# Cross attention of a six-layer decoder: sequences taken in pairs, and the 257th key folded in as a shift

## The chip, the cores and the metric

The kernel runs on one core of a Trainium2 chip. The metric is device time in microseconds (us) of one launch; lower is better.

## The reference, cut to what matters

The program is a stack of twelve blocks over 32 sequences of 32 tokens with 256 features. The fourth block is a decoder of six layers, and the change lies in it alone:

```python
def mha(xq, xkv, W, B, mask):            # H = 16 heads of DH = 16
    q, k, v = proj(xq, W[0], B[0]), proj(xkv, W[1], B[1]), proj(xkv, W[2], B[2])
    score = jnp.einsum('bhqd,bhkd->bhqk', q, k) / math.sqrt(DH)
    if mask is not None:
        score = jnp.where(mask[:, None] == 0, -10000.0, score)
    attn = jax.nn.softmax(score, axis=-1)
    out = jnp.einsum('bhqk,bhkd->bhqd', attn, v)
    ...
    return out @ W[3] + B[3]

def step(x, p):                          # six times
    x = layer_norm(mha(x, x, saw, sab, mask) + x, ...)
    x = layer_norm(mha(x, enc, caw, cab, None) + x, ...)
    x = layer_norm(relu(x @ W1 + B1) @ W2 + B2 + x, ...)
```

`enc` is the context, 257 keys for each sequence (2 x 128 and one more). All is fp32.

## The kernel before, in words

`decoder_layers` writes out by hand one schedule for five engines. The 32 sequences are eight tiles of four sequences (128 token rows); with six layers that makes 48 positions. The schedule is a software pipeline: each step of its main loop works on four positions at once, one in self attention ("sa"), one in the projections of the context ("prep"), one in cross attention ("ca"), and one in the output projection and the MLP ("out", "dm"). A step has eight units, u = 0 to 7, one for each half of the heads (cc) and each sequence (j) of the "ca" position.

In each unit TensorE does, in this order: `scores` of the unit (into banks 0 and 1 of PSUM), `transposes` of the unit before (into bank 2), the jobs that `UNIT_JOBS[u]` lists, and `values` of the unit two before (into bank 3). Jobs take the four banks of a ring in turn; job n waits until job n-4's bank has been evacuated by the engine that the list names. The kinds of job named below: K and V project keys and values of the context, S0 to S7 are self attention's stages, D0 transposes the MLP's input, D1 and D2 are its first matmuls in two halves, D3 is its second matmul (it waits for ScalarE's evacuation of D1 and D2), Y is the output projection of cross attention, X and XK project the 257th value and key of all sequences once a layer.

VectorE (DVE in the rows) takes the maximum of each score row (`maxima`), evacuates its jobs (`take`), turns sums into reciprocals (`reciprocals`, every fourth unit), assembles heads (`own_heads`, u = 1 and 5) and does self attention's shift (`self_shift`, u = 3) and shares (`self_shares`, u = 4). ScalarE (ACT) does `exponentials`, then `copy_transposed` (bank 2 to SBUF), then its evacuations of the unit, among them D0's (one copy) and D1's and D2's (four activations each). Each engine works through its own list strictly in order, so a wait holds whatever stands behind it.

The wait that orders scores against the softmax, and the one that orders the second MLP matmul, read:

```python
need(pe, "exp_done", 2 * k)              # scores: banks 0 and 1 are read out
...
need_evacuated(pe, pos, "D1", 0)         # job D3
need_evacuated(pe, pos, "D2", 1)
```

## Time and profile before

| | |
|---|---|
| median of 3 runs | 4612.44 us (4609.56 to 4612.98) |
| profiled execution, its own time | 4595.03 us |
| its span | 4593.2 us |
| TensorE (PE) busy | 4045.7 us, 88% of the span |
| VectorE (DVE) busy | 2613.4 us, 57% |
| ScalarE (ACT) busy | 1853.6 us, 40% |
| GpSimd (POOL) busy | 300.9 us, 7% |
| mean granted TensorE clock | 0.937 of full speed |

Busy time is the time in which an engine has at least one instruction under way. PE is the matmul side of TensorE, PEld its weight loads. Instructions on TensorE overlap, so the time that one group takes from the queue is read from the start of the group to the start of the next, not from its own duration. A matmul in fp32 stands as two instructions in the trace. The decoder's score matmuls run from 774 to 2816 us of the span.

### The profile page before, as it was taken

To read this page: it belongs to the slowest core of one execution; us is meant where nothing else is said; L and a number is where in the kernel's file an instruction comes from. 1 tells how busy PE (TensorE), PEld (TensorE's weight loads), DVE (VectorE), ACT (ScalarE), POOL (GpSimd) and SP (SyncE) were. 2 spreads that over 40 slices of the span, in tenths; PEclk is the share of its full clock that TensorE was granted. 3 is DMA by queue.
4 is the path that set the end of the run, shared out by engine and by line. 5 is a ranking of instruction groups with operands and counts; after the bars stand their busy time and mean duration, and the time that the engine had idled before them with its cause. 6 is when DMAs were issued, how large, how long until landed. Compare 5 with 4: busy or idle time off the path is not lost. (4 is left out here: it accounts for less than half of the span.)

```text
span 4593.2 us, 105087 instructions
## 1 busy us (share of the span) xinstructions
PE 4045.7 (88%) x43842; PEld 3101.4 (68%) x43842; DVE 2613.4 (57%) x5580; ACT 1853.6 (40%) x5080; POOL 300.9 (7%) x560
## 2 busy tenths in 40 slices
PE   7988995999999999999999997779588787888867
PEld 6766884777777777777777775568345577566635
DVE  3435115777777777777777774721367654345545
ACT  1221221444444444444444443212266454255523
POOL 0000101000000000000000000010211000000000
PEclk9998997999999999999999998879799888888878
DMA  4110573011111111111111100048544300000000
GB/s 148 59 58 3 203 288 99 29 33 43 51 33 43 51 35 41 51 35 40 51 35 40 51 29 9 3 160 293 172 153 145 116 0 0 25 30 28 11 1 12
DMA packets 116921, 310.54 MB, mean 68 GB/s; under 512 B 29352, under 2 KB 75625, under 8 KB 92017
## 3 DMA queue, kind: packets, MB, share of 16 engines
q1 hardware_dynamic: 113392, 295.61, 18.8%
q0 software_dynamic: 3072, 8.39, 0.5%
q8 instruction: 342, 5.60, 0.5%
q14 instruction: 115, 0.93, 0.1%
HBM read 289.01 MB, written 14.94 MB: 66 GB/s over the span
## 5 line engine op out<-in xcount | busy, mean ns | idle before, releaser
L2490 ACT ACTIVATE layers_probs<-banks,layers_negmax 128x257 f32<-128x257 f32 x768 | 357.6, 471 | 1002.7 <-DVE layers_negmax L2369 1002.7
L2213 PE MATMUL banks<-ctx_tiles,weights_a 128*128 128x257 f32 x1536 | 397.4, 381 | 0.0
L2219 PE MATMUL banks<-weights_a,ctx_tiles 128*128 128x256 f32 x1536 | 379.4, 380 | 0.0
L2219 PEld LDWEIGHTS banks<-weights_a,ctx_tiles 128*128 128x128 f32 x1536 | 285.1, 191 | 35.4
L2369 DVE TENSOR_REDUCE layers_negmax<-banks 128x2 f32<-128x514 f32 x384 | 262.3, 683 | 71.5 <-PE banks L2274 71.5
L2213 PEld LDWEIGHTS banks<-ctx_tiles,weights_a 128*128 128x128 f32 x1536 | 270.9, 191 | 26.6 <-ACT layers_KT L2467 0.4
L2274 PE MATMUL banks<-layers_KT,layers_qblk 32*64 32x257 f32 x3072 | 256.2, 403 | 26.6 <-ACT layers_probs L2490 26.3
L2282 PEld LDWEIGHTS banks<-const,layers_probs 128*128 128x128 f32 x1536 | 162.2, 141 | 149.4 <-issue 149.3
L2282 PE MATMUL banks<-const,layers_probs 128*128 128x128 f32 x1536 | 253.6, 288 | 0.0
L2349 DVE TENSOR_TENSOR layers_V<-banks,rows_a 128x256 f32<-128x256 f32 x384 | 160.2, 418 | 138.8 <-PE banks L2219 132.9
L2495 ACT COPY layers_pT<-banks 128x512 f32<-128x512 f32 x384 | 223.5, 582 | 3.3 <-PE banks L2282 3.3
L2467 ACT ACTIVATE layers_KT<-banks,layers_ca_bk 128x257 f32<-128x257 f32 x384 | 184.2, 496 | 47.8 <-PE banks L2213 47.7
L2258 PE MATMUL banks<-layers_dm_nT,weights_b 128*128 128x128 f32 x1536 | 189.3, 277 | 0.6 <-ACT layers_dm_nT L2464 0.6
L2258 PEld LDWEIGHTS banks<-layers_dm_nT,weights_b 128*128 128x128 f32 x1536 | 184.8, 194 | 3.2 <-ACT layers_dm_nT L2464 0.9
L2263 PE MATMUL banks<-weights_b,layers_hid 128*128 128x256 f32 x768 | 173.8, 379 | 1.7 <-ACT layers_hid L2481 1.7
L2294 PEld LDWEIGHTS banks<-layers_pT,layers_V 128*32 128x32 f32 x6144 | 109.7, 109 | 87.8 <-issue 78.0
L2294 PE MATMUL banks<-layers_pT,layers_V 128*32 128x64 f32 x6144 | 163.6, 224 | 0.3 <-ACT layers_pT L2495 0.3
L2263 PEld LDWEIGHTS banks<-weights_b,layers_hid 128*128 128x128 f32 x768 | 145.7, 190 | 21.7 <-issue 2.1
L2490 ACT ACTIVATION_READ_ACCUMULATOR layers_probs<-banks,layers_negmax 128x1 f32 x768 | 150.6, 196 | 0.0
L2274 PEld LDWEIGHTS banks<-layers_KT,layers_qblk 32*64 32x64 f32 x3072 | 79.5, 130 | 96.4 <-issue 39.4
L2772 PE MATMUL banks<-weights_a,ctx_tiles 128*128 128x512 f32 x256 | 129.8, 636 | 1.0 <-DVE l2x_own L2847 0.5
L2345 DVE SCALAR_TENSOR_TENSOR weights_a<-banks,layers_sa_cols,const 128x1024 f32<-128x1024 f32 x96 | 118.4, 1274 | 7.3 <-PE banks L2206 7.3
(695 smaller groups left out, 8329.3 us busy)
## 6 DMA issues: line engine op xcount, KB each, us to landing
ctx_tiles<-in_ctx SPq DMA_DIRECT2D x65, 1028.0 KB, 5.1
weights_a<-in_L_w SPq DMA_DIRECT2D x44, 1024.0 KB, 5.4
l2x_B<-positions SPq DMA_DIRECT2D x32, 1280.0 KB, 5.9
weights_b<-in_L_w SPq DMA_DIRECT2D x32, 1024.0 KB, 6.2
weights_c<-in_L_w SPq DMA_DIRECT2D x16, 1024.0 KB, 7.1
weights_b<-in_L_xattn_w SPq DMA_DIRECT2D x12, 1024.0 KB, 7.4
l0x_key_rows<-in_ctx_rows SPq DMA_DIRECT2D x32, 256.0 KB, 2.7
ctx_tiles<-in_ctx_keys SPq DMA_DIRECT2D x32, 256.0 KB, 2.8
```

The costliest lines, as they stand in the source:

```text
L2213: last = mm(o[:, 0:LK], ca_wk[:, c, m * P:(m + 1) * P], E.ctx[:, tile % 2, c, j * LK:(j + 1) * LK], start=c == 0, stop=c == DC - 1)
L2219: last = mm(o[:, 0:D], E.ctx[:, tile % 2, c, first:first + P], ca_wv[:, c], start=c == 0, stop=c == DC - 1)
L2258: last = mm(o[:, i * P:(i + 1) * P], dm_w1[:, c, m * P:(m + 1) * P], dm_nT[:, c], start=c == 0, stop=c == DC - 1)
L2263: last = mm(o[:, 0:D], hid[:, m], dm_w2[:, m], start=m == 0, stop=m == FC - 1)
L2274: last = mm(ps[half, r // 2, 0:LK], qblk[rows, tile % 2, cc, j], KT[rows, tile % 2, cc, j * LK:(j + 1) * LK], start=True, stop=True)
L2282: last = tr(ps[:, TURN, (KC * t + c) * P:(KC * t + c + 1) * P], probs[:, cc, j, t, 1 + c * P:1 + (c + 1) * P], E.c("ident"))
L2294: last = mm(ps[32 * i:32 * (i + 1), PV, j * 64:(j + 1) * 64], V[:, pos % 2, KC * j + c, cc * P + 32 * i:cc * P + 32 * (i + 1)], pT[:, k % ...
L2349: last = v.tensor_tensor(V[:, tile % 2, arg], o[:, 0:D], E.rA[:, 0], ALU.add)
L2369: v.tensor_reduce(negmax[:, k % 2], ps[:, 0:2, 0:LK], AX.X, ALU.max, negate=True).then_inc(s["max_ready"], 1)
L2467: last = a(KT[:, pos % 2, m, j * LK:(j + 1) * LK], o[:, 0:LK], ACT.Identity, bias=ca_bk[:, m:m + 1])
L2490: a(probs[:, cc, j, t], ps[:, t, 0:LK], ACT.Exp, bias=negmax[:, k % 2, t:t + 1], accum_out=totals[:, cc, t, j:j + 1]).then_inc(s["exp_done ...
L2495: nc.scalar.copy(pT[:, k % 2].rearrange("p t c x -> p (t c x)"), ps[:, TURN]).then_inc(s["copied"], 1)
```

## The change

What it does:

- The key projections leave out the 257th key. It is projected once a layer for all sequences (job XK), and its projection is subtracted from every other key as the bias of the evacuation; the scores are then differences against the last key, whose own exponential is exp(-max), taken once for four sequences (`last_e`). The maximum is held at 0 or above by a second, tiny DVE instruction.
- K and V jobs cover two blocks of 256 columns each and fill a bank: four K and four V jobs a step instead of eight and eight.
- Scores, maxima and exponentials are done for two sequences at once, in even units. Transposes and values stay per sequence, but values of two sequences stand together in odd units. There are four buffers of `pT` instead of two.
- ScalarE's order in a unit is now `copy_transposed`, `exponentials` (even units: four of them, and in units 2 and 6 also `last_e`), evacuations. VectorE evacuates S6 in its own unit instead of in the next one, and takes put-off jobs ahead of `maxima`.

The diff, without the hunks that only rename what a semaphore waits for:

```diff
@@ -2042,2 +2042,3 @@
     VC = GB * KC
+    KW = KC * P
     U = DC * GB
...
@@ -2052,12 +2053,12 @@
     UNIT_JOBS = [
-        [k_job(0), v_job(0), k_job(1), v_job(1), ("S0", None, "act")],
-        [("S1q", None, "dve"), k_job(2), ("S1k", None, "act"), k_job(3), ("n", None, "act")],
-        [("q", None, "act"), k_job(4), ("Y", None, "dve"), ("S3", None, "dve")],
-        [k_job(5), v_job(2), k_job(6)],
-        [("D0", None, "act"), v_job(3), v_job(4), v_job(5)],
-        [("S2", None, "dve"), ("D1", 0, "act"), k_job(7), v_job(6), ("S6", None, "dve")],
-        [("D2", 1, "act"), v_job(7), ("X", None, "act")],
+        [("XK", None, "act"), ("S0", None, "act"), k_job(0), v_job(0)],
+        [("S1q", None, "dve"), k_job(1), ("S1k", None, "act"), ("n", None, "act")],
+        [("q", None, "act"), v_job(1), ("Y", None, "dve"), ("S3", None, "dve")],
+        [k_job(2), v_job(2)],
+        [("D0", None, "act"), k_job(3), ("S2", None, "dve")],
+        [("D1", 0, "act"), v_job(3), ("S6", None, "dve")],
+        [("D2", 1, "act"), ("X", None, "act")],
         [("S7", None, "dve"), ("D3", None, "dve")],
     ]
-    PART = {"n": "prep", "X": "prep", "q": "prep", "K": "prep", "V": "prep", "Y": "out", "S0": "sa", "S1q": "sa", "S1k": "sa", "S2": "sa", "S3": "sa", "S6": "sa", "S7": "sa",
+    PART = {"n": "prep", "X": "prep", "XK": "prep", "q": "prep", "K": "prep", "V": "prep", "Y": "out", "S0": "sa", "S1q": "sa", "S1k": "sa", "S2": "sa", "S3": "sa", "S6": "sa", "S7": "sa",
             "D0": "dm", "D1": "dm", "D2": "dm", "D3": "dm"}
...
@@ -2082,7 +2083,8 @@
         nT, qT, qblk = sb("nT", [DC, P]), sb("qT", [DC, P]), sb("qblk", [2, DC, GB, 2 * LQ])
-        KT, V = sb("KT", [2, DC, CT]), sb("V", [2, VC, D])
-        probs, pT = sb("probs", [DC, GB, 2, LK]), sb("pT", [2, 2, KC, P])
-        negmax, totals, spread = sb("negmax", [2, 2]), sb("totals", [2, 2, GB]), sb("spread", [2, 2, GB, LQ])
+        KT, V = sb("KT", [2, DC, GB * KW]), sb("V", [2, VC, D])
+        probs, pT = sb("probs", [DC, GB, 2, KW]), sb("pT", [4, 2, KC, P])
+        negmax, totals, spread = sb("negmax", [DC, 2, GB]), sb("totals", [2, 2, GB]), sb("spread", [2, 2, GB, LQ])
         blend, attnT = sb("blend", [2, GB, LQ]), sb("attnT", [DC, P])
         rates, last_v = sb("rates", [2, 2, GB]), sb("last_v", [2, DC, NB])
+        last_e, last_k, less_last = sb("last_e", [DC, 2, GB]), sb("last_k", [DC, NB]), sb("less_last", [2, DC, NB])
         sa_nT, sa_k, sa_v = sb("sa_nT", [DC, P]), sb("sa_k", [DC, P]), sb("sa_v", [GB, D])
...
@@ -2207,3 +2209,3 @@
                     elif kind == "K":
-                        m, j = arg
+                        m, i = arg
                         if arg == (0, 0):
@@ -2212,9 +2214,16 @@
                         for c in range(DC):
-                            last = mm(o[:, 0:LK], ca_wk[:, c, m * P:(m + 1) * P], E.ctx[:, tile % 2, c, j * LK:(j + 1) * LK], start=c == 0, stop=c == DC - 1)
+                            keys = E.ctx[:, tile % 2, c].rearrange("p (j k) -> p j k", j=GB)[:, 2 * i:2 * i + 2, 1:LK]
+                            last = mm(o.rearrange("p (j k) -> p j k", j=2), ca_wk[:, c, m * P:(m + 1) * P], keys, start=c == 0, stop=c == DC - 1)
                     elif kind == "V":
-                        first = arg // KC * LK + 1 + arg % KC * P
                         if arg == 0:
                             need_weights(pe, "w_ca_v", pos)
-                        for c in range(DC):
-                            last = mm(o[:, 0:D], E.ctx[:, tile % 2, c, first:first + P], ca_wv[:, c], start=c == 0, stop=c == DC - 1)
+                        for b in range(KC):
+                            first = arg * LK + 1 + b * P
+                            for c in range(DC):
+                                last = mm(o[:, b * D:(b + 1) * D], E.ctx[:, tile % 2, c, first:first + P], ca_wv[:, c], start=c == 0, stop=c == DC - 1)
+                    elif kind == "XK":
+                        need_weights(pe, "w_ca_k", pos)
+                        for m in range(DC):
+                            for c in range(DC):
+                                last = mm(o[:, m * NB:(m + 1) * NB], ca_wk[:, c, m * P:(m + 1) * P], E.last[:, c], start=c == 0, stop=c == DC - 1)
                     elif kind == "X":
@@ -2269,7 +2278,8 @@
                         pe.wait_ge(s["qblk_ready"], pos + 1)
-                        need_evacuated(pe, pos, "K", (DC - 1, GB - 1))
+                        need_evacuated(pe, pos, "K", (DC - 1, 1))
                     need(pe, "exp_done", 2 * k)
-                    for r in (0, 2, 1, 3):
-                        rows, half = slice(32 * r, 32 * (r + 1)), slice(64 * (r % 2), 64 * (r % 2 + 1))
-                        last = mm(ps[half, r // 2, 0:LK], qblk[rows, tile % 2, cc, j], KT[rows, tile % 2, cc, j * LK:(j + 1) * LK], start=True, stop=True)
+                    for a in range(2):
+                        for r in (0, 2, 1, 3):
+                            rows, half = slice(32 * r, 32 * (r + 1)), slice(64 * (r % 2), 64 * (r % 2 + 1))
+                            last = mm(ps[half, r // 2, a * KW:(a + 1) * KW], qblk[rows, tile % 2, cc, j + a], KT[rows, tile % 2, cc, (j + a) * KW:(j + a + 1) * KW], start=True, stop=True)
                     last.then_inc(s["scores_done"], 1)
...
@@ -2290,6 +2300,6 @@
                         if cc == 0:
-                            need_evacuated(pe, pos, "V", VC - 1)
+                            need_evacuated(pe, pos, "V", GB - 1)
                     for c in range(KC):
                         for i in range(4):
-                            last = mm(ps[32 * i:32 * (i + 1), PV, j * 64:(j + 1) * 64], V[:, pos % 2, KC * j + c, cc * P + 32 * i:cc * P + 32 * (i + 1)], pT[:, k % 2, i // 2, c, 64 * (i % 2):64 * (i % 2 + 1)], start=c == 0, stop=c == KC - 1)
+                            last = mm(ps[32 * i:32 * (i + 1), PV, j * 64:(j + 1) * 64], V[:, pos % 2, KC * j + c, cc * P + 32 * i:cc * P + 32 * (i + 1)], pT[:, k % 4, i // 2, c, 64 * (i % 2):64 * (i % 2 + 1)], start=c == 0, stop=c == KC - 1)
                     last.then_inc(s["pv_done"], 1)
@@ -2302,10 +2312,11 @@
                 for it in range(N * U):
-                    if ca_unit(it):
+                    if it % 2 == 0 and ca_unit(it):
                         scores(*ca_unit(it))
-                    if ca_unit(it - 1):
-                        transposes(*ca_unit(it - 1))
+                    if ca_unit(it - 2):
+                        transposes(*ca_unit(it - 2))
                     for a in jobs_in(it):
                         job(*a)
-                    if ca_unit(it - 2):
-                        values(*ca_unit(it - 2))
+                    for back in (3, 2):
+                        if it % 2 and ca_unit(it - back):
+                            values(*ca_unit(it - back))
 
...
@@ -2367,4 +2378,6 @@
                 def maxima(k, pos, cc, j):
-                    dve.wait_ge(s["scores_done"], k + 1)
-                    v.tensor_reduce(negmax[:, k % 2], ps[:, 0:2, 0:LK], AX.X, ALU.max, negate=True).then_inc(s["max_ready"], 1)
+                    dve.wait_ge(s["scores_done"], k // 2 + 1)
+                    peak = negmax[:, cc, :, j:j + 2]
+                    link(v.tensor_reduce(peak, ps[:, 0:2].rearrange("p t (a x) -> p t a x", a=2), AX.X, ALU.max, negate=True))
+                    v.tensor_scalar(peak, peak, 0.0, None, ALU.min).then_inc(s["max_ready"], 1)
 
@@ -2372,4 +2385,6 @@
                     need(dve, "exp_done", 2 * (k + 1))
-                    link(v.reciprocal(rates[:, :, 0], totals[:, cc]))
-                    link(v.tensor_tensor(rates[:, :, 1], rates[:, :, 0], probs[:, cc, :, :, 0].rearrange("p j t -> p t j"), ALU.mult))
+                    dve.wait_ge(s["last_exp"], k // GB + 1)
+                    link(v.tensor_tensor(rates[:, :, 0], totals[:, cc], last_e[:, cc], ALU.add))
+                    link(v.reciprocal(rates[:, :, 0], rates[:, :, 0]))
+                    link(v.tensor_tensor(rates[:, :, 1], rates[:, :, 0], last_e[:, cc], ALU.mult))
                     v.tensor_tensor(spread[:].rearrange("p t s j q -> p (t s j) q"), E.c("pick").unsqueeze(1).to_broadcast([P, 4 * GB, LQ]),
@@ -2417,4 +2432,2 @@
                     step, u = it // U, it % U
-                    if ca_unit(it):
-                        maxima(*ca_unit(it))
                     for a in put_off:
@@ -2422,4 +2435,6 @@
                     put_off.clear()
+                    if it % 2 == 0 and ca_unit(it):
+                        maxima(*ca_unit(it))
                     for a in jobs_in(it):
-                        if a[3] in ("S3", "S6", "D3"):
+                        if a[3] in ("S3", "D3"):
                             put_off.append(a)
@@ -2465,4 +2480,15 @@
                     elif kind == "K":
-                        m, j = arg
-                        last = a(KT[:, pos % 2, m, j * LK:(j + 1) * LK], o[:, 0:LK], ACT.Identity, bias=ca_bk[:, m:m + 1])
+                        m, i = arg
+                        for j in (2 * i, 2 * i + 1):
+                            seq = pos % NG * GB + j
+                            last = a(KT[:, pos % 2, m, j * KW:(j + 1) * KW], o[:, j % 2 * KW:(j % 2 + 1) * KW], ACT.Identity, bias=less_last[:, pos // NG % 2, m, seq:seq + 1])
+                    elif kind == "XK":
+                        for m in range(DC):
+                            a(last_k[:, m], o[:, m * NB:(m + 1) * NB], ACT.Identity, bias=ca_bk[:, m:m + 1]).then_inc(s["last_keys"], 1)
+                        act.wait_ge(s["last_keys"], DC * (pos // NG + 1))
+                        for m in range(DC):
+                            last = a(less_last[:, pos // NG % 2, m], last_k[:, m], ACT.Identity, scale=-1.0, bias=ca_bk[:, m:m + 1])
+                        last.then_inc(s["evac_act"], 1)
+                        need_evacuated(act, pos, "XK")
+                        return
                     elif kind == "q":
@@ -2484,8 +2510,11 @@
                 def exponentials(k, pos, cc, j):
-                    act.wait_ge(s["max_ready"], k + 1)
-                    need(act, "transposed", k - U + 1)
+                    act.wait_ge(s["max_ready"], k // 2 + 1)
+                    need(act, "transposed", k + 1 - U + 1)
                     if j == 0:
                         need(act, "spread_ready", k // GB - 1)
-                    for t in range(2):
-                        a(probs[:, cc, j, t], ps[:, t, 0:LK], ACT.Exp, bias=negmax[:, k % 2, t:t + 1], accum_out=totals[:, cc, t, j:j + 1]).then_inc(s["exp_done"], 1)
+                    for i in (j, j + 1):
+                        for t in range(2):
+                            a(probs[:, cc, i, t], ps[:, t, i % 2 * KW:(i % 2 + 1) * KW], ACT.Exp, bias=negmax[:, cc, t, i:i + 1], accum_out=totals[:, cc, t, i:i + 1]).then_inc(s["exp_done"], 1)
+                    if j == GB - 2:
+                        a(last_e[:, cc], negmax[:, cc], ACT.Exp).then_inc(s["last_exp"], 1)
 
@@ -2493,4 +2522,4 @@
                     act.wait_ge(s["transposed"], k + 1)
-                    need(act, "pv_done", k - 1)
-                    nc.scalar.copy(pT[:, k % 2].rearrange("p t c x -> p (t c x)"), ps[:, TURN]).then_inc(s["copied"], 1)
+                    need(act, "pv_done", k - 3)
+                    nc.scalar.copy(pT[:, k % 4].rearrange("p t c x -> p (t c x)"), ps[:, TURN]).then_inc(s["copied"], 1)
 
@@ -2498,6 +2527,6 @@
                     step, u = it // U, it % U
-                    if ca_unit(it):
+                    if ca_unit(it - 2):
+                        copy_transposed(*ca_unit(it - 2))
+                    if it % 2 == 0 and ca_unit(it):
                         exponentials(*ca_unit(it))
-                    if ca_unit(it - 1):
-                        copy_transposed(*ca_unit(it - 1))
                     for b in jobs_in(it):
```

Two places of the order. First ScalarE in unit 4 (the copy out of bank 2, the exponentials, the evacuation of D0 to `dm_nT`, then D1's to `hid`). Before:

```order
L2507 ACTIVATE layers_sa_sc<-layers_sa_sc 128x512
L2490 ACTIVATE layers_probs,layers_totals<-banks,layers_negmax 128x257 x2
L2495 COPY layers_pT<-banks 128x512
L2464 COPY layers_dm_nT<-banks 128x256
L2490 ACTIVATE layers_probs,layers_totals<-banks,layers_negmax 128x257 x2
L2495 COPY layers_pT<-banks 128x512
L2481 ACTIVATE layers_hid<-banks,layers_dm_cols 128x128 x4
```

And in the changed kernel, through unit 6, where the second half of the MLP's hidden layer (D2) is evacuated:

```order
L2536 ACTIVATE layers_sa_sc<-layers_sa_sc 128x512
L2524 COPY layers_pT<-banks 128x512
L2517 ACTIVATE layers_probs,layers_totals<-banks,layers_negmax 128x256 x4
L2479 COPY layers_dm_nT<-banks 128x256
L2484 ACTIVATE layers_KT<-banks,layers_less_last 128x256 x2
L2524 COPY layers_pT<-banks 128x512
L2507 ACTIVATE layers_hid<-banks,layers_dm_cols 128x128 x4
L2524 COPY layers_pT<-banks 128x512
L2517 ACTIVATE layers_probs,layers_totals<-banks,layers_negmax 128x256 x4
L2519 ACTIVATE layers_last_e<-layers_negmax 128x8
L2507 ACTIVATE layers_hid<-banks,layers_dm_cols 128x128 x4
```

D0's evacuation stood behind two exponentials and a copy, and stands behind four exponentials; D2's stood behind two and a copy, and stands behind five.

Second VectorE from unit 5 to the maxima of unit 6 (V's evacuation, S6's in L2357 and L2360 of before, own heads from L2386 of before on, the maximum). Before:

```order
L2349 TENSOR_TENSOR layers_V<-banks,rows_a 128x256
L2386 TENSOR_SCALAR layers_blend<-banks,const 128x128
L2387 TENSOR_TENSOR layers_blend<-banks,layers_last_v 128x128
L2388 SCALAR_TENSOR_TENSOR layers_blend<-banks,const,layers_blend 128x128
L2389 TENSOR_TENSOR layers_blend<-banks,layers_blend 128x128
L2390 TENSOR_TENSOR layers_attnT<-layers_blend 128x128
L2369 TENSOR_REDUCE layers_negmax<-banks 128x2
L2357 TENSOR_SCALAR layers_sa_blend<-banks,const,layers_sa_bv 128x128 x2
L2360 SCALAR_TENSOR_TENSOR layers_sa_attnT<-banks,const,layers_sa_blend 128x128 x2
```

In the changed kernel:

```order
L2360 TENSOR_TENSOR layers_V<-banks,rows_a 128x512
L2368 TENSOR_SCALAR layers_sa_blend<-banks,const,layers_sa_bv 128x128 x2
L2371 SCALAR_TENSOR_TENSOR layers_sa_attnT<-banks,const,layers_sa_blend 128x128 x2
L2401 TENSOR_SCALAR layers_blend<-banks,const 128x128
L2402 TENSOR_TENSOR layers_blend<-banks,layers_last_v 128x128
L2403 SCALAR_TENSOR_TENSOR layers_blend<-banks,const,layers_blend 128x128
L2404 TENSOR_TENSOR layers_blend<-banks,layers_blend 128x128
L2405 TENSOR_TENSOR layers_attnT<-layers_blend 128x128
L2381 TENSOR_REDUCE layers_negmax<-banks 128x2x2
L2382 TENSOR_SCALAR layers_negmax<-layers_negmax 128x2x2
```

S6's four instructions moved from behind unit 6's maximum to ahead of it, and the maximum covers twice the columns.

## Rows read from the trace of the kernel before

**Rows 1.** Windows, decoder: us; PE, PEld, DVE, ACT, POOL busy (count), clock, DMA share, GB/s.

```profile
774.00:2816.00 2042.00, 1988.19 (x22373) 1527.14 (x22372) 1471.12 (x3283) 939.86 (x3045) 115.90 (x280) 1.00 0.12 39
```

**Rows 2.** Timeline of one step, PE: start us, us, engine, line, operation.

```profile
1716.93 0.66 PE L2274 MATMUL banks<-layers_KT,layers_qblk 32*64 32x257 f32 x8
...
1727.43 0.44 PE L2199 MATMUL banks<-const,h_state 128*128 128x128 f32 x2 [0.51 <-DVE weights_a L2345]
...
1727.79 0.43 PE L2294 MATMUL banks<-layers_pT,layers_V 128*32 128x64 f32 x16
...
1728.04 0.62 PE L2299 MATMUL banks<-layers_spread,const 128*32 128x256 f32 x8
...
1738.21 0.66 PE L2274 MATMUL banks<-layers_KT,layers_qblk 32*64 32x257 f32 x8 [0.39 <-ACT layers_probs L2490]
...
1738.80 0.66 PE L2282 MATMUL banks<-const,layers_probs 128*128 128x128 f32 x4
...
1739.52 2.76 PE L2219 MATMUL banks<-weights_a,ctx_tiles 128*128 128x256 f32 x12
...
1742.20 0.43 PE L2294 MATMUL banks<-layers_pT,layers_V 128*32 128x64 f32 x16
...
1742.56 0.66 PE L2274 MATMUL banks<-layers_KT,layers_qblk 32*64 32x257 f32 x8
...
1748.12 1.10 PE L2246 MATMUL banks<-layers_sa_pT,layers_sa_v 128*32 128x64 f32 x64
...
1750.90 1.95 PE L2258 MATMUL banks<-layers_dm_nT,weights_b 128*128 128x128 f32 x16
...
1759.86 0.66 PE L2274 MATMUL banks<-layers_KT,layers_qblk 32*64 32x257 f32 x8
```

**Rows 3.** Timeline of the same step, DVE.

```profile
1737.96 0.77 DVE L2403 COPY_PREDICATED_SCALAR layers_sa_sc<-mask_zero,layers_floor 128x512 f32 x1
...
1740.09 0.68 DVE L2369 TENSOR_REDUCE layers_negmax<-banks 128x2 f32<-128x514 f32 x1
...
1746.63 1.21 DVE L2351 TENSOR_TENSOR layers_sa_v<-banks,const 128x1024 f32<-128x1024 f32 x1
...
1750.02 0.35 DVE L2386 TENSOR_SCALAR layers_blend<-banks,const 128x128 f32<-128x128 f32 x1 [1.36 <-PE banks L2299]
...
1751.53 0.68 DVE L2369 TENSOR_REDUCE layers_negmax<-banks 128x2 f32<-128x514 f32 x1
...
1752.13 0.72 DVE L2357 TENSOR_SCALAR layers_sa_blend<-banks,const,layers_sa_bv 128x128 f32<-128x128 f32 x2
...
1752.88 0.61 DVE L2360 SCALAR_TENSOR_TENSOR layers_sa_attnT<-banks,const,layers_sa_blend 128x128 f32<-128x128 f32 x2
```

**Rows 4.** Timeline of the same step, ACT.

```profile
1742.19 0.39 ACT L2464 COPY layers_dm_nT<-banks 128x256 f32<-128x256 f32 x1
...
1752.24 0.48 ACT L2490 ACTIVATE layers_probs<-banks,layers_negmax 128x257 f32<-128x257 f32 x1 [2.60 <-DVE layers_negmax L2369]
...
1753.16 0.58 ACT L2495 COPY layers_pT<-banks 128x512 f32<-128x512 f32 x1
...
1753.62 1.16 ACT L2481 ACTIVATE layers_hid<-banks,layers_dm_cols 128x128 f32<-128x128 f32 x4
```

**Rows 5.** Timeline, PE, the decoder's first step, two waits.

```profile
780.19 0.44 PE L2199 MATMUL banks<-const,h_state 128*128 128x128 f32 x2 [1.75 <-ACT layers_KT L2467]
...
804.93 1.10 PE L2246 MATMUL banks<-layers_sa_pT,layers_sa_v 128*32 128x64 f32 x64 [1.53 <-DVE layers_sa_v L2351]
```

**Rows 6.** Windows around those two waits, columns as in rows 1.

```profile
777.40:780.90 3.50, 1.75 (x15) 0.98 (x13) 1.94 (x5) 1.99 (x7) 0.00 (x0) 1.00 0.00 0
780.90:784.30 3.40, 3.40 (x21) 2.95 (x14) 0.78 (x2) 1.64 (x6) 0.00 (x0) 0.50 0.00 0
802.40:805.80 3.40, 1.87 (x67) 1.44 (x69) 2.75 (x4) 1.87 (x6) 0.00 (x0) 1.00 0.00 0
805.80:809.20 3.40, 3.29 (x73) 1.95 (x62) 2.29 (x7) 0.17 (x1) 0.00 (x0) 1.00 0.02 5
```

16 lines of the change are left out of this document (8 added, 8 removed).

## The prediction, made before the changed kernel ran

> **What bounds the kernel now.** I read the page first, then the windows over the decoder, the timeline of one step on each engine, and the waits. In the decoder TensorE has work under way for 1988 of 2042 us at full clock; DVE stands at 1471 and ACT at 940 [rows 1]. One step goes from the scores at 1716.93 to those at 1759.86, 42.93 us, and there are 48. Inside it TensorE waits twice: 0.51 us for DVE before a transpose and 0.39 us for exponentials before scores [rows 2]. So TensorE's own queue sets the step, and ACT's and DVE's chains fit behind it. The decoder gains where that queue gets shorter, and loses where one of those chains, made longer, comes out ahead of it.
>
> All sums are against the profiled execution (span 4593.2, its own time 4595.0 us); the median of the runs is 4612.4, 17 us more. I add the change to the median.
>
> **What gets shorter on TensorE.** The columns stay: leaving out the 257th saves one column in 257. What goes is switching between shapes. Single `values` take 0.36 us to the scores behind them (1742.20 to 1742.56), and 0.25 where the next matmuls have the same shape (1727.79 to 1728.04) [rows 2]; so two `values` in a row take about 0.36 + 0.22 = 0.58 instead of 0.72, and entering the shape from wide matmuls, about 0.1, is paid once instead of twice. Scores take 0.59 (1738.21 to 1738.80). Their eight instructions run four abreast, two waves; two more waves cost at least the column rate, 0.22 each (12 instructions of 256 columns in 2.68 us with one switch, 1739.52 to 1742.20), and at most another 0.59: a pair is 1.03 to 1.18, and I take 1.03, since the added waves have no switch. Transposes behind wide matmuls lose about 0.06. Per pair: 0.15 + 0.14 + 0.1 + 0.06 = 0.45, per step 1.8 us. Both waits of before are in units whose order changes; I take them as gone, 0.9, and 0.15 for the restart (estimate). The least here is 1.2 us (scores without gain), the most 2.85.
>
> Here a rule can be set against the rows. K's 16 matmuls of 257 columns become 8 of 512. Sixteen instructions of 128 columns take 1.95 us, 12 of 256 columns 2.68 [rows 2]: twice the columns, twice the time, so the number of instructions is worth next to nothing and I count nothing. The Trainium skill (TensorEngine Tiling (Array Packing), Instruction Overhead) gives each matmul about 60 cycles of overhead; by it the 16 instructions saved in a step would give another 0.4 us, and the forecast would be some 19 us lower. The rows decide.
>
> XK adds 8 instructions once a layer, which load 128 columns each: about 0.11 us apiece as in [rows 2] (1750.90), 0.9 us, 5 us over six layers. The tiny new operations on DVE and ACT (minimum, `last_e`, one more in `reciprocals`) cost some 0.2 us each on engines with room, except where they stand in the chains below.
>
> **What gets longer: two chains.** Pair maximum: 1024 columns take DVE 1.21 us (1746.63) [rows 3]; with the minimum chained behind it, 1.42 from its start to its release. ACT starts 0.03 later (1751.53 + 0.68 against 1752.24), and two exponentials take 0.92 (1752.24 to 1753.16) [rows 3, 4], so four take 1.84. Before, an evacuation stood behind two; now it stands behind all four, and these behind a maximum twice as long.
>
> *Unit 4, D0 to D1.* Count from the start of unit 4's scores. V2's evacuation ends at about +0.15 (it begins about with the `values` ahead and covers 512 columns). Then comes self attention's shift, 2.13 us (1737.96 to 1740.09) [rows 3], to +2.27, and only then the maximum: released +3.69, exponentials +3.72 to +5.56, D0's copy 0.39 [rows 4] to +5.95, TensorE released at +6.00. TensorE itself is there earlier: scores 1.03, transposes and D0 0.72 (1738.80 to 1739.52), K 1.72, S2 0.86, unit 5's transposes 0.44, in all 4.77 [rows 2]. D1 waits 1.23 us. In the old order D0's copy had two exponentials ahead of it, and three V jobs, values, the next scores and S2 stood between D0 and D1 on TensorE; now it is K3 and S2.
>
> *Unit 6, D2 to D3.* Count from the start of unit 6's scores. S6's last result comes 0.18 after the `values` behind it start (1748.12 + 1.10) [rows 2], about 0.8 us before the scores. Its evacuation, 1.36 us (1752.13 to 1753.49), no longer waits until after the maximum; it ends at +0.59. Own heads take 1.51 (1750.02 to 1751.53) [rows 3]: +2.10. Maximum and minimum +3.52, exponentials +3.55 to +5.39, `last_e` +5.54, D2's four activations 1.16 [rows 4] to +6.70, D3 may start at +6.75. TensorE is there at 1.03 + 0.50 + 1.78 (D2) + 0.44 + 0.86 (S7) = +4.61. D3 waits 2.14 us. V7, which stood in unit 6, is gone from there. Behind D3 on TensorE are `values` and the next step's scores, so nothing gives this time back.
>
> The other waits I went through hold: S1q behind S0's copy has 0.7 us to spare, K2 behind q's evacuation 0.3 us (late next, if anything is), S6 behind self attention's shares 0.2 us. The context loads start earlier than before, with V3 in unit 5. No weight transfer is moved in SP's queue, and the weights of K are asked for in unit 5, many us ahead of XK.
>
> Sum per step: -1.8 - 1.05 + 1.23 + 2.14 = +0.5 us, 48 times 25 us; with XK about +29 us: 4641.
>
> **The clock.** A wait of some 2 us has a second price. In the decoder's first step TensorE waited 1.75 us, then ran at a granted clock of 0.50, that is 1.2 GHz, for the next 3.4 us; after a wait of 1.53 us in a stretch just as dense it stayed at 1.00, 2.4 GHz [rows 5, 6]. D3's wait has 2.14 us by starts, 1.97 idle. I expect it to cost the clock in some steps and not in others, since the drop comes at moments of its own, not at once. 3.4 us at half speed lose 1.7 us of TensorE's work, and D3, 16 matmuls without a pause, stands right there. Half of the steps: 24 times 1.7, another 41 us. Together +70: **4682 us**.
>
> The Trainium skill (TensorE: Matmul & The Clock Gate, Why this matters for your kernels) accepts idle gaps longer than this one between bursts; by it the clock would hold and the time be 4641. The wait of 1.75 us in the rows speaks against it.
>
> **The rivals.**
> 1. *Both waits, the clock falls after many of the long ones* (forecast): 4682, chance 0.42. Its own range 4655 to 4715.
> 2. *Both waits, the clock holds.* 4641 (4622 to 4655), chance 0.25. For it: 1.97 us is an estimate, with an error of some 0.4, and 1.53 did no harm.
> 3. *The waits are there but smaller, about what TensorE saves:* new waits of 2.6 to 2.95 us in a step instead of 3.4, and no loss of clock. 4605 to 4622, chance 0.10.
> 4. *Faster:* TensorE's shorter queue wins. The mechanism would be one place: D3 finds D2's evacuation done early, because own heads and the maximum in unit 6 start sooner than I reckon (if S6's evacuation and own heads cost 0.8 us less than their rows). The point from which it decides: new waits under 2.55 us in a step. With D3's wait at 1.2 us the step gains 0.42 us, 20 us in all, less 5 for XK: 4597. If both waits vanished, -2.85 x 48 + 5 = -132 us: 4480. Chance 0.13; for it speaks that the work saved is certain and the waits are worked out, against it that 0.8 us must be found.
> 5. *The clock falls in nearly every step,* or a pair of scores costs 1.18 and q's evacuation comes late too: 48 times 1.7 us, 4723, and with 0.3 us a step more 4738. Chance 0.10.
>
> About 0.2% (9 us) is what a measurement of this kernel can tell from no change: slower 0.77, within it 0.10, faster 0.13. The range leaves out the far ends of cases 4 and 5: 4598 to 4730.
>
> **What the profile would show.** Right: in each of the 48 steps a wait of D1's matmuls for `dm_nT` and one of D3's for `hid`, near 1.2 and 2 us; stretches of 3.4 us at clock 0.50 within the decoder, most of them behind D3's wait; four score groups of 16 instructions to a step with 1.03 us to the next group; none of the old waits before transposes and scores. Wrong: TensorE without waits, or steps shorter than 42.9 us. My weakest points are the length of D3's wait, which rests on a chain of seven durations, and the number of steps in which the clock falls.

## The result, and the profile after

The changed kernel takes 4680.99 us (median of 4 runs, 4672.28 to 4687.78), the kernel before 4611.00 in the same comparison (4 runs): a ratio of 1.0152 with a 95% interval of 1.0133 to 1.0172, 70 us slower. The forecast was 4682, slower.

The page of the profiled execution of the changed kernel (its own time 4682.26 us): span, then busy time and share of the engines, then the granted clock in 40 slices.

```profile
span 4680.5 us, 103588 instructions
...
PE 4025.6 (86%) x43122; PEld 3004.6 (64%) x43122; DVE 2628.4 (56%) x5484; ACT 1875.9 (40%) x5200; POOL 300.4 (6%) x560
...
PEclk9998997999999999999999998969799888888878
```

TensorE works 20 us less than before and the span is 87 us longer. Not all of the 87 us belong to the change. This is the decoder's first matmul, with the wait ahead of it:

```profile
737.92 0.66 PE L2201 MATMUL banks<-const,h_state 128*128 128x128 f32 x2 [33.79 <-PEq L201]
```

In the trace of before the same instruction starts at 726.87, so 11 us of the difference between these two executions lie ahead of the decoder, where nothing was changed, and 6 us lie behind it. From the first step's scores to the 48th step's it is 2077.3 us against 2014.1, +63.2; the decoder's start and end add about 7. That makes the 70 us of the medians.

One step on TensorE, from the end of unit 2 to unit 1 of the next step (start us, us, engine, line, operation; it answers to [rows 2]):

```profile
1728.67 1.07 PE L2247 MATMUL banks<-weights_a,layers_sa_k 128*32 128x256 f32 x16
1729.67 0.66 PE L2292 MATMUL banks<-const,layers_probs 128*128 128x128 f32 x4
...
1734.29 1.09 PE L2284 MATMUL banks<-layers_KT,layers_qblk 32*64 32x256 f32 x16
1735.31 0.66 PE L2292 MATMUL banks<-const,layers_probs 128*128 128x128 f32 x4
...
1736.02 1.88 PE L2216 MATMUL banks<-ctx_tiles,weights_a 128*128 128x512 f32 x4
1737.74 1.03 PE L2241 MATMUL banks<-weights_c,layers_sa_nT 128*128 128x256 f32 x4
1738.61 0.60 PE L2292 MATMUL banks<-const,layers_probs 128*128 128x128 f32 x4
1740.35 2.02 PE L2267 MATMUL banks<-layers_dm_nT,weights_b 128*128 128x128 f32 x16 [1.15 <-ACT layers_dm_nT L2479]
...
1745.94 1.09 PE L2284 MATMUL banks<-layers_KT,layers_qblk 32*64 32x256 f32 x16
...
1749.68 1.03 PE L2260 MATMUL banks<-weights_c,layers_sa_attnT 128*128 128x256 f32 x4
1752.64 5.38 PE L2272 MATMUL banks<-weights_b,layers_hid 128*128 128x256 f32 x16 [1.93 <-ACT layers_hid L2507]
1757.95 0.66 PE L2304 MATMUL banks<-layers_pT,layers_V 128*32 128x64 f32 x32
1758.54 1.09 PE L2284 MATMUL banks<-layers_KT,layers_qblk 32*64 32x256 f32 x16
```

The reader is to see: a pair of scores (L2284) leaves TensorE's queue after 1.02 us; in unit 5 the transposes at 1738.61 are followed by nothing until D1 (L2267) at 1740.35; in unit 7 S7 (L2260) starts at 1749.68 and D3 (L2272) only at 1752.64, after 1.93 us idle; and D3's 16 instructions then take 5.31 us to the values behind them, where they took 3.62 in other steps.

VectorE in the same step (answers to [rows 3]):

```profile
1736.56 1.22 DVE L2381 TENSOR_REDUCE layers_negmax<-banks 128x4 f32<-128x1024 f32 x1
1737.81 0.17 DVE L2382 TENSOR_SCALAR layers_negmax<-layers_negmax 128x4 f32<-128x4 f32 x1
...
1745.21 0.73 DVE L2368 TENSOR_SCALAR layers_sa_blend<-banks,const,layers_sa_bv 128x128 f32<-128x128 f32 x2 [0.38 <-PE banks L2255]
...
1746.49 0.34 DVE L2401 TENSOR_SCALAR layers_blend<-banks,const 128x128 f32<-128x128 f32 x1
...
1747.99 1.22 DVE L2381 TENSOR_REDUCE layers_negmax<-banks 128x4 f32<-128x1024 f32 x1
```

ScalarE in the same step (answers to [rows 4]):

```profile
1738.02 0.47 ACT L2517 ACTIVATE layers_probs<-banks,layers_negmax 128x256 f32<-128x256 f32 x1 [0.24 <-DVE layers_negmax L2382]
...
1739.83 0.38 ACT L2479 COPY layers_dm_nT<-banks 128x256 f32<-128x256 f32 x1
...
1749.44 0.47 ACT L2517 ACTIVATE layers_probs<-banks,layers_negmax 128x256 f32<-128x256 f32 x1 [1.20 <-DVE layers_negmax L2382]
...
1751.35 1.15 ACT L2507 ACTIVATE layers_hid<-banks,layers_dm_cols 128x128 f32<-128x128 f32 x4
```

Both chains can be read off. Unit 4: the maximum starts at 1736.56, 2.27 us behind the scores at 1734.29; it is released at 1737.98; four exponentials take from 1738.02 to 1739.83; D0's copy (`dm_nT`) ends at 1740.21, and D1 starts at 1740.35. Unit 6: S6's evacuation (1745.21) and own heads (1746.49) come ahead of the maximum at 1747.99, 2.05 us behind the scores at 1745.94; the exponentials start at 1749.44, D2's evacuation (`hid`) ends at 1752.50, D3 starts at 1752.64.

The window behind D3's start (busy us and count of PE, PEld, DVE, ACT, POOL, then clock, DMA share and GB/s), and who TensorE waited for between the first and the last step:

```profile
1753.80:1757.20 3.40, 3.40 (x9) 2.66 (x8) 0.80 (x2) 0.00 (x0) 0.00 (x0) 0.50 0.36 90
```

```profile
PE banks L2272 <- ACT layers_hid L2507: 78.0, 45, 1.9
PE banks L2267 <- ACT layers_dm_nT L2479: 46.8, 41, 1.2
...
PE banks L2309 <- issue: 4.1, 3, 1.4
PE banks L2284 <- issue: 2.4, 3, 1.2
```

Two waits stand where before there were none. D1's is there in 46 of the 47 intervals between steps, at 1.10 to 1.15 us idle in all but the last (in five of them, left out of the lines above, another releaser is named). D3's is 1.93 us idle in 34 intervals and mostly shorter in the others, where a layer begins or TensorE was late for another reason. A granted clock of 0.50, that is 1.2 GHz, stands right behind D3's start in 13 of these 34; such an interval is 45.41 us long, a plain one 43.72. The kernel before has 42.93 in all but the first two, the last and the five with a new layer.

### The profile page after: what moved, and what is told of

It reads as the page before. It is cut to its first block and busy times, and to the rows that moved or that the text cites. A ratio compares the mean times of both kernels' runs of the same rounds, so it can differ in the third digit from the quotient of the medians.

```text
span 4680.5 us, 103588 instructions
## 1 busy us (share of the span) xinstructions
PE 4025.6 (86%) x43122; PEld 3004.6 (64%) x43122; DVE 2628.4 (56%) x5484; ACT 1875.9 (40%) x5200; POOL 300.4 (6%) x560
## 3 DMA queue, kind: packets, MB, share of 16 engines
q1 hardware_dynamic: 113392, 295.61, 18.5%
## 5 line engine op out<-in xcount | busy, mean ns | idle before, releaser
L2517 ACT ACTIVATE layers_probs<-banks,layers_negmax 128x256 f32<-128x256 f32 x768 | 353.2, 472 | 134.7 <-DVE layers_negmax L2382 134.7
L2216 PE MATMUL banks<-ctx_tiles,weights_a 128*128 128x512 f32 x768 | 363.4, 596 | 0.0
L2272 PE MATMUL banks<-weights_b,layers_hid 128*128 128x256 f32 x768 | 200.8, 421 | 84.2 <-ACT layers_hid L2507 84.2
L2360 DVE TENSOR_TENSOR layers_V<-banks,rows_a 128x512 f32<-128x512 f32 x192 | 132.6, 691 | 241.8 <-PE banks L2223 241.8
L2267 PE MATMUL banks<-layers_dm_nT,weights_b 128*128 128x128 f32 x1536 | 195.1, 282 | 55.5 <-ACT layers_dm_nT L2479 50.0
L2272 PEld LDWEIGHTS banks<-weights_b,layers_hid 128*128 128x128 f32 x768 | 158.3, 211 | 126.1 <-issue 86.9
L2381 DVE TENSOR_REDUCE layers_negmax<-banks 128x4 f32<-128x1024 f32 x192 | 233.9, 1218 | 6.5 <-PE banks L2284 3.1
L2484 ACT ACTIVATE layers_KT<-banks,layers_less_last 128x256 f32<-128x256 f32 x384 | 163.9, 486 | 158.6 <-PE banks L2216 158.6
L2267 PEld LDWEIGHTS banks<-layers_dm_nT,weights_b 128*128 128x128 f32 x1536 | 183.3, 196 | 65.7 <-DVE layers_sa_v L2362 60.8
L2284 PE MATMUL banks<-layers_KT,layers_qblk 32*64 32x256 f32 x3072 | 213.0, 390 | 2.6 <-issue 2.4
L2216 PEld LDWEIGHTS banks<-ctx_tiles,weights_a 128*128 128x128 f32 x768 | 131.9, 192 | 92.8 <-issue 92.8
L2284 PEld LDWEIGHTS banks<-layers_KT,layers_qblk 32*64 32x64 f32 x3072 | 98.8, 132 | 78.2 <-issue 45.3
L2507 ACT ACTIVATE layers_hid<-banks,layers_dm_cols 128x128 f32<-128x128 f32 x384 | 109.9, 378 | 54.5 <-PE banks L2267 54.5
L2304 PE MATMUL banks<-layers_pT,layers_V 128*32 128x64 f32 x6144 | 126.4, 223 | 4.0 <-ACT layers_pT L2524 4.0
```

The lines of the kernel that those rows point to most:

```text
L2216: last = mm(o.rearrange("p (j k) -> p j k", j=2), ca_wk[:, c, m * P:(m + 1) * P], keys, start=c == 0, stop=c == DC - 1)
L2267: last = mm(o[:, i * P:(i + 1) * P], dm_w1[:, c, m * P:(m + 1) * P], dm_nT[:, c], start=c == 0, stop=c == DC - 1)
L2272: last = mm(o[:, 0:D], hid[:, m], dm_w2[:, m], start=m == 0, stop=m == FC - 1)
L2284: last = mm(ps[half, r // 2, a * KW:(a + 1) * KW], qblk[rows, tile % 2, cc, j + a], KT[rows, tile % 2, cc, (j + a) * KW:(j + a + 1) * KW], ...
L2304: last = mm(ps[32 * i:32 * (i + 1), PV, j * 64:(j + 1) * 64], V[:, pos % 2, KC * j + c, cc * P + 32 * i:cc * P + 32 * (i + 1)], pT[:, k % ...
L2360: last = v.tensor_tensor(V[:, tile % 2, KC * arg:KC * (arg + 1)], o.rearrange("p (b d) -> p b d", b=KC), E.rA[:, 0].unsqueeze(1).to_broadc ...
```

## The experiments

Ratios are to the kernel before, timed on the same chip. The chips differ between groups of rows, so two ratios whose intervals overlap are told apart by the traces, not by the ratios. "Steps" is the time from the first step's scores to the 48th step's in the profiled execution, "plain step" the most frequent interval among those without a D3 at half clock. Expectations given as times are on the footing of the result, where the kernel before took 4611 us; a measured ratio times 4611 can be held against them.

| kernel | ratio (95% interval) | plain step, us | steps, us |
|---|---|---|---|
| before | 1 | 42.93 | 2014.1 |
| changed | 1.0152 (1.0133 to 1.0172) | 43.72 | 2077.3 |
| first evacuation first, unit 4 only | 1.0144 (1.0124 to 1.0165) | 43.46 | 2069.9 |
| S7 twice | 1.0124 (1.0103 to 1.0145) | 43.73 | 2059.6 |
| S6 put off | 1.0104 (1.0087 to 1.0121) | 43.40 | 2048.3 |
| heads late | 1.0037 (1.0022 to 1.0051) | 42.86 | 2022.9 |
| first evacuation first, unit 6 only | 0.9939 (0.9919 to 0.9959) | 41.81 | 1980.0 |
| first evacuation first, all even units | 0.9880 (0.9855 to 0.9905) | 41.55 | 1956.0 |
| both orders mended, values single | 0.9808 (0.9786 to 0.9829) | 41.03 | 1926.7 |
| both orders mended | 0.9768 (0.9752 to 0.9784) | 40.42 | 1897.8 |

### ScalarE's order, in all even units

```diff
+                    own = [b for b in jobs_in(it) if b[5] == "act"]
+                    early = own[:1] if u in (0, 2, 4, 6) else []
+                    for b in early:
+                        take(*b)
                     if it % 2 == 0 and ca_unit(it):
                         exponentials(*ca_unit(it))
-                    for b in jobs_in(it):
+                    for b in own[len(early):]:
                         take(*b)
```

Expected: 

> The changed kernel, but ScalarE takes the first evacuation of an even unit ahead of the pair's exponentials. Theory (ScalarE's order makes both waits, 1.3 us before D1 and 2.1 us before D3): both waits go and with D3's wait the loss of clock. D1's wait comes back in part as a wait of S6 for self attention's shares on VectorE, about 1.1 us, because in the changed kernel these were ready only 0.2 us ahead of S6. Step 43.72 - 0.2 - 2.1 = 41.4 us, total 4681 - 110 - 27 (clock) = about 4544. If nothing replaces D1's wait: 4490. Rival (the later, longer maximum on VectorE holds the step, whatever ScalarE's order is): the exponentials, now later still, hold scores or transposes, and the step stays near 43.7, total 4670 or more.

Measured: ratio 0.9880 (4556 us on the footing of the expectation), plain step 41.55 us. The largest waits of TensorE from the second step on:

```profile
PE banks L2255 <- DVE layers_sa_pT L2427: 46.8, 44, 1.2
PE banks L2267 <- issue: 1.4, 1, 1.4
```

D1's wait is gone, D3's is 0.18 us by starts, and S6 (L2255) waits 1.1 us for self attention's shares, as worked out. No D3 ran at half clock. The exponentials, now later in units 4 and 6, hold no matmul in these steps. The rival falls.

### The same in unit 4 alone, and in unit 6 alone

```diff
-                    early = own[:1] if u in (0, 2, 4, 6) else []
+                    early = own[:1] if u in (4,) else []
```

These lines are against the experiment above. In the second kernel the last line has `(6,)`.

Expected for unit 4: 

> Only in unit 4 the evacuation of D0 goes ahead of the exponentials. Theory: D1's wait of 1.3 us goes, a wait of about 1.1 us stands before S6, the step gains 0.2 us, D3's wait and the loss of clock stay: 4671. Rival (each wait is a cost of its own): the step gains 1.3 us, 62 us in all: 4619.

Measured: ratio 1.0144 (4677 us on that footing), plain step 43.46, 0.26 us less.

```profile
PE banks L2272 <- ACT layers_hid L2507: 81.2, 45, 2.5
PE banks L2255 <- DVE layers_sa_pT L2427: 46.7, 44, 1.2
```

D1's wait is gone and S6's is there in its place; D3's (L2272) is unchanged. D3 is at half clock in 19 steps here, 13 in the changed kernel, with the same wait ahead of it: six times 1.69 us, which takes back 10 of the 12 us that 0.26 us a step give. Removing the shorter wait alone gives next to nothing: VectorE's queue stands right behind it, and the clock fell more often.

Expected for unit 6: 

> Only in unit 6 the evacuation of D2 goes ahead of the exponentials. Theory: D3's wait of 2.1 us goes and no D3 runs at half clock, D1's wait stays: 4681 - 101 - 27 = 4553. Rival (the clock falls for another reason than D3's wait): 4681 - 101 = 4580, with slow stretches left.

Measured: ratio 0.9939 (4583 us on that footing), plain step 41.81, 1.91 us less.

```profile
PE banks L2267 <- ACT layers_dm_nT L2479: 45.8, 40, 1.2
PE banks L2309 <- issue: 5.9, 4, 1.8
```

D3's wait falls from 2.10 us by starts to 0.18 (D2's evacuation still ends a little late), D1's stays, and no D3 runs at half clock. The time lies 30 us above the theory's 4553 and beside the rival's 4580; what excludes the rival is the trace, which has no slow stretch left behind the first step. The steps got 97 us shorter, where 1.91 x 47 and 22 us for the clock make 112. The 15 us that are missing: the pauses of TensorE that the last section tells of lengthen the steps by 13 us here and by 5 in the changed kernel, where D3's wait swallowed part of them; the five steps with a new layer lose 3 us in the same way, and the first interval is 1.7 us longer here.

Units 4 and 6 alone gain 0.26 and 1.91 us, all even units together 2.17: units 0 and 2, where the order was changed too, add nothing.

### More work inside D3's wait

```diff
-                        for c in range(DC):
-                            last = mm(o[:, 0:D], sa_attnT[:, c], sa_wo[:, c], start=c == 0, stop=c == DC - 1)
+                        for again in range(2):
+                            for c in range(DC):
+                                last = mm(o[:, 0:D], sa_attnT[:, c], sa_wo[:, c], start=c == 0, stop=c == DC - 1)
```

Expected: 

> The matmuls of S7 are done twice into the same bank, 0.87 us of idle work for TensorE that lies within D3's wait; the result is the same. Theory (D3's wait of 2.1 us costs the clock): the wait falls to 1.2 us, step lengths stay at 43.72 but no step has a D3 at half clock: 4681 - 27 = 4654. Rival 1 (the clock falls whatever TensorE's pause is): 4681. Rival 2 (added work is paid in full): 4681 + 42 = 4723.

Measured: ratio 1.0124 (4668 us on that footing), plain step 43.73. TensorE's waits, and D3's instructions in this kernel and in the changed one (min/median/max ns):

```profile
PE banks L2268 <- ACT layers_dm_nT L2480: 45.8, 40, 1.2
PE banks L2273 <- ACT layers_hid L2508: 41.1, 44, 1.1
```

```profile
L2273 PE MATMUL banks<-weights_b,layers_hid x720: 379/379/454, 860.3 to 2798.6; 128*128 128x256 f32 x180
```

```profile
L2272 PE MATMUL banks<-weights_b,layers_hid x720: 379/379/671, 867.9 to 2826.6; 128*128 128x256 f32 x180
```

With 0.87 us of extra matmuls in each step the 48 steps took 17.7 us less (one profiled execution each; the intervals of the two ratios overlap by a little). The plain step is as long as in the changed kernel, the wait is 1.1 us idle instead of 1.9, and in this window no D3 instruction comes near the 671 ns that the slowest took at half clock. The one D3 behind the window, in the last step, waited 2.47 us idle and did run at half clock. By this the loss of clock is an effect of D3's long wait, and it cost 22 us (13 times 1.69), not the 27 that the expectation had counted with. Both rivals fall: the first by the trace, since the time lies midway between it and the theory, the second by the step.

### VectorE's part in D3's wait

Own heads behind unit 6's maximum:

```diff
                     if it % 2 == 0 and ca_unit(it):
                         maxima(*ca_unit(it))
+                    if u == 6 and ca_unit(it - 3):
+                        own_heads(*ca_unit(it - 3))
...
-                    if ca_unit(it - 2) and (it - 2) % GB == GB - 1:
+                    if u == 1 and ca_unit(it - 2):
                         own_heads(*ca_unit(it - 2))
```

Expected: 

> The changed kernel, but VectorE assembles the first half's heads after unit 6's maximum instead of before it (ScalarE's order as in the changed kernel). Theory (VectorE's 1.5 us of own heads and S6's evacuation stand in the chain to D3's wait): the maximum starts 0.95 us earlier, D3's wait falls from 2.1 to 1.2 us, no D3 at half clock: -46 - 27 us against the changed kernel, ratio to before 0.999. Rival (the wait comes from ScalarE's order alone, VectorE is not in it): D3's wait and the clock stay, ratio 1.015.

Measured: ratio 1.0037, plain step 42.86, 0.86 us less where 0.95 was expected, and no D3 at half clock. The ratio came out above the 0.999 expected: the steps got 54 us shorter, not 73. The clock gave back 22 us and not 27, the wait 40 and not 46, and pauses lengthen the steps by 11 us here, 5 in the changed kernel.

```profile
PE banks L2267 <- ACT layers_dm_nT L2481: 47.0, 41, 1.2
PE banks L2272 <- ACT layers_hid L2509: 43.2, 45, 1.1
```

S6's evacuation behind unit 6's maximum, as before the change:

```diff
+                    late = [a for a in put_off if a[3] == "S6"]
                     for a in put_off:
-                        take(*a)
+                        if a[3] != "S6":
+                            take(*a)
                     put_off.clear()
                     if it % 2 == 0 and ca_unit(it):
                         maxima(*ca_unit(it))
+                    for a in late:
+                        take(*a)
                     for a in jobs_in(it):
-                        if a[3] in ("S3", "D3"):
+                        if a[3] in ("S3", "S6", "D3"):
```

Expected: 

> The changed kernel, but S6's evacuation on VectorE stands behind unit 6's maximum again, as in the kernel before. Theory: own heads start 0.45 us earlier, D2's evacuation ends 0.45 us earlier; S7 on TensorE now waits about 0.7 us for S6's evacuation, and D3 about 1 us after it, both within the same span. The step gains 0.45 us (22 us in all), and with two short waits instead of one of 2.1 us no D3 runs at half clock, another 27: ratio to before 1.004. Rival (the clock falls as often): 1.010. Rival (S6's place is of no account): 1.015.

Measured: ratio 1.0104, plain step 43.40: 0.32 us less, where 0.45 was expected.

```profile
PE banks L2272 <- ACT layers_hid L2511: 31.9, 45, 0.7
PE banks L2260 <- DVE layers_sa_attnT L2371: 23.0, 36, 0.7
```

The one wait is split in two of 0.65 and 0.72 us, and no D3 of the steps ran at half clock. The forecast of 1.004 missed: 29 us were gained in the steps, not 49. The ratio is that of the first rival (the clock falls as often), but the trace excludes it. Both runs together say that VectorE's queue ahead of the maximum is part of D3's wait, but moving it can't undo it: the exponentials alone keep D2's evacuation back.

### Both orders mended

Self attention's shares ahead of the reciprocals, on top of ScalarE's order:

```diff
+                    if u == 4 and steps[step]["sa"] is not None:
+                        self_shares(steps[step]["sa"])
                     if ca_unit(it - 1):
                         if (it - 1) % GB == GB - 1:
                             reciprocals(*ca_unit(it - 1))
...
-                    if u == 4 and steps[step]["sa"] is not None:
-                        self_shares(steps[step]["sa"])
```

Expected: 

> Both: ScalarE takes the first evacuation of an even unit ahead of the exponentials, and VectorE does self attention's shares in unit 4 ahead of the reciprocals. Theory (with D1's wait gone, the 1.1 us that S6 waits are VectorE's queue in unit 4, and the reciprocals' 1.25 us ahead of the shares make them): no wait before S6, step 41.55 - 1.1 = 40.45 us, time 53 us under that of the kernel with the order of ScalarE alone, a ratio to the kernel before of 0.976 to 0.977. Rival (the reciprocals, now later, hold the matmuls that spread them in unit 5): the wait only moves there, ratio 0.988.

Measured: ratio 0.9768, plain step 40.42. TensorE's waits of over 0.15 us from the second step on, of which there is one, and five rows of units 5 to 7:

```profile
PE banks L2272 <- ACT layers_hid L2507: 0.9, 1, 0.9
```

```profile
1704.42 1.95 PE L2267 MATMUL banks<-layers_dm_nT,weights_b 128*128 128x128 f32 x16
1706.21 1.89 PE L2223 MATMUL banks<-weights_a,ctx_tiles 128*128 128x256 f32 x8
1708.03 1.10 PE L2255 MATMUL banks<-layers_sa_pT,layers_sa_v 128*32 128x64 f32 x64
...
1713.68 1.03 PE L2260 MATMUL banks<-weights_c,layers_sa_attnT 128*128 128x256 f32 x4
1714.73 3.69 PE L2272 MATMUL banks<-weights_b,layers_hid 128*128 128x256 f32 x16
```

This is the change as it could have been: 2.3% faster than the kernel before, and 3.8% faster than the changed one, from two changes of order that touch no instruction's work. What was between is seen here as its absence: D1 at 1704.42 to V3 to S6 without a gap, and 1.05 us from S7 to D3 instead of 2.96.

### What the fewer changes of shape are worth

```diff
-                    for back in (3, 2):
-                        if it % 2 and ca_unit(it - back):
-                            values(*ca_unit(it - back))
+                    if ca_unit(it - 2):
+                        values(*ca_unit(it - 2))
```

Expected: 

> The kernel with both orders mended (ScalarE's first evacuation ahead, self attention's shares ahead of the reciprocals), step 40.42 us without a wait, but the values of each sequence stand in their own unit again instead of two together in odd units. Same matmuls, only more changes of shape. Theory (TensorE's gain in the changed kernel is fewer changes of shape): 0.14 us for each of four pairs, about 0.1 for entering the shape from wide matmuls in units 0, 4 and 6 and about 0.06 for leaving it there, together 1.0 us a step, 48 us: ratio to the kernel before 0.987. Rival (changes of shape cost nothing beyond the matmuls; the gain came from elsewhere): step 40.4, ratio 0.977.

Measured: ratio 0.9808, plain step 41.03: 0.61 us more than with values in pairs, where 1.0 was expected.

```profile
1712.13 0.43 PE L2304 MATMUL banks<-layers_pT,layers_V 128*32 128x64 f32 x16
1712.49 0.66 PE L2292 MATMUL banks<-const,layers_probs 128*128 128x128 f32 x4
...
1717.40 0.43 PE L2304 MATMUL banks<-layers_pT,layers_V 128*32 128x64 f32 x16
1717.76 1.09 PE L2284 MATMUL banks<-layers_KT,layers_qblk 32*64 32x256 f32 x16
```

The values at 1712.13 take 0.36 us to the transposes behind them, and the values ahead of scores 0.36, as in the kernel before. So changes of shape cost time, and the rival falls. Laid side by side, the two traces show which of the four pairs saves: joining unit 0's values with unit 1's, and unit 4's with unit 5's, is worth 0.3 us each, as expected. Unit 2's are worth nothing, since they stand behind S3, which has their shape already: S3 takes 0.89 us to the values, and 1.01 to the transposes when the values are gone. Of unit 6's next to nothing is left, since with pairs TensorE reaches D3 earlier and waits there for D2's evacuation, 0.18 us by starts.

## Why the prediction was right, point by point

**What bounds the kernel.** TensorE's queue set the step; this held. With both orders mended only D3's 0.18 us are left and the step is 40.42 us, all but the changed queue's own length.

**What TensorE saves.** A pair of scores took 1.02 us (1.03 forecast) and a pair of values 0.58 to 0.59 (0.58). The sum of 1.8 us a step was too high. S3 is now followed by transposes instead of values, a change of shape that was not there before (1.00 us from S3 at 1728.67 to the transposes, 0.89 to the values before), and entering the values from wide matmuls is spared in three units of four. From 42.93, less 1.13 for the old waits by starts, to 40.42 less the 0.18 that D3 still waits there, it is 1.56 us. This term of the sum was mis-sized, by 0.24 us a step.

**The number of instructions.** Four K instructions of 512 columns take 1.72 us (1736.02 to 1737.74), as eight of 257 did. Columns are what is paid for here; the 0.4 us a step that the Trainium skill's overhead for each matmul (TensorEngine Tiling (Array Packing), Instruction Overhead) would have given, by estimate, are not there.

**Unit 4, D0 to D1.** Forecast 1.23 us, measured 1.31 by starts (1.74 from the transposes, of which they take 0.44). Maximum to release 1.42 (1.42), exponentials 1.81 (1.84). The experiment in unit 4 shows that ScalarE's order makes this wait, and that the 0.2 us named as S6's room behind the shares were about right: it gained 0.26.

**Unit 6, D2 to D3.** Forecast 2.14 us, measured 2.10 by starts. ScalarE's order makes it: mended in unit 6 alone, the kernel is faster than before. On VectorE, putting S6's evacuation behind the maximum takes 0.32 us off the step, putting own heads there 0.86.

**The clock.** That some of these waits cost the clock and others not was right, and the price too, 1.69 us (1.7). The number was half of the forecast: 13 intervals, not 24, so 22 us instead of 41.

**The sum.** The plain step grew by 0.79 us where 0.52 was forecast: 37 us in all against 25. The clock took 22 us against 41. XK, forecast at 5 us, took next to nothing: the step in which a layer begins is 0.84 us longer than a plain one, 0.81 in the kernel before, for its matmuls lie inside D3's wait, which is 1.08 us idle there (where D3 hardly waits, a layer's step is 1.44 us longer). Two terms were not in the forecast at all: the pauses of the last section, 5 us, and the decoder's start and end, 7 us. The total of 4682 against 4681 is right to a microsecond by luck, because these errors cancel; its parts are right to about 20 us.

**The rivals.** The second (the clock holds) lies 40 us below the measured time and is excluded by the half-clock stretches. The third falls with it: the new waits are 3.41 us by starts in a plain step, above its 2.95. The fifth is excluded by the 13 intervals and by the pair of scores at 1.02 us. Of the fourth: own heads moved out of the chain do what it says to D3's wait (1.23 us by starts), and the time still came out 0.37% above the kernel before, not below. The plain step is 0.07 us shorter than before where it forecast 0.42: TensorE saves 1.56 us and not 1.8, and the waits are a little longer. The pauses, 11 us, more than undo that.

## What to carry to other kernels

When work is done in pairs, each engine's turn at it is twice as long, and what stands behind it in that engine's list gets twice as late: put the short evacuation that the busiest engine waits for ahead of the long batch. It cost 2.7% here to do it the other way round, on an engine that is busy 40% of the time, and 3.8% together with one more place of the same kind on VectorE.

When a wait is removed, look at what was due just behind it: D1's wait gave back 0.26 of its 1.31 us until VectorE's order was mended as well. And a wait of about 2 us on TensorE may cost more than itself, since the clock can fall behind it (13 times in 34 here); filling it with matmuls that nobody needs made the decoder's steps shorter.

## What the runs showed of the hardware that was not expected

The clock falls behind some of several equal waits. D3 waits 1.93 us idle in 34 steps of the changed kernel, and 13 of them are followed by half clock; with unit 4 alone mended it is 19 of 37. At 1.0 to 1.1 us idle (S7 twice, heads late) no D3 had it. Between the two, a pause of 1.70 us in the second step of the kernel with all even units mended was followed by half clock, and one of 1.75 us in the same place with unit 4 alone mended was not. Which waits it falls behind doesn't look like chance: the fall comes 0.1 to 1.1 us after D3's start, and in the kernel with unit 4 alone mended the first five of these distances are 0.40, 0.54, 0.64, 0.78 and 0.92 us, the next five 0.14, 0.23, 0.36, 0.50 and 0.53. Nothing was run to find out what decides.

TensorE also pauses where the profile names no releaser, in a few steps, often in the middle of a run of equal instructions:

```profile
1258.67 0.59 PE L2309 MATMUL banks<-layers_spread,const 128*32 128x256 f32 x3
1260.61 0.63 PE L2309 MATMUL banks<-layers_spread,const 128*32 128x256 f32 x5 [1.35 <-issue]
```

In the changed kernel there are seven such pauses with 6.9 us together between the first and last step, in the one with unit 6 alone mended seven with 8.8 us. S7 twice has six, heads late eight, S6 put off seven, the two in which unit 4's order is mended (unit 4 only, all even units) three each; the kernel before and the two with both orders mended have none. It is not an accident of one execution: in the changed kernel, the one with unit 6 alone mended, heads late and S6 put off, pauses stand in the same six intervals, counted from the first step: numbers 8, 21 and 34, and 11, 24 and 37, each time 13 apart.

The trace has one thing that stands ahead of every one of them. The page lists a DMA queue named `instruction` (packets, MB, share); its packets have 16 KB each:

```profile
q8 instruction: 337, 5.52, 0.5%
```

The pause above ends at 1260.61; the last packet of this queue before it ran from 1257.91 to 1259.05, and the one before that had come 20.8 us earlier, where the median distance in this kernel is 11.9. All 41 pauses of the seven kernels end 1.2 to 1.6 us after such a packet has landed, and the packet came 16.8 to 20.8 us after the one before. In the three kernels without pauses no distance from the second step on is above 18.5 us. So it looks as if TensorE had run out of instructions; that is read from these times, and was not tested. Why the packets come late in these steps stays open. In 35 of the 41 the load of the next context tile had been issued in the 7 us before; the change brought that load forward to V3, but it is just as early in the kernels with both orders mended, which don't pause, so the load alone does not explain them.
